# A recommender tower (CIN and three dense layers): group 0 as four batches by 32 columns a tile, its first tile from the first gather alone, w1's quarters sent behind gathers, 17 warm-up products

## The reference

```
e = stack([tbl_0[ids[:, 0]], ..., tbl_31[ids[:, 31]]], axis=1)     # b, field, d
x0 = prev = e
for W in (filter_0, filter_1):                                     # 1024 x 128, 4096 x 128
    z = einsum('bhd,bmd->bhmd', x0, prev).reshape(b, h * m, d)
    prev = relu(einsum('bpd,pn->bnd', z, W[0]))
    outs.append(prev)
z = sum(concatenate(outs, axis=1), axis=-1)                        # b, 256
h = maximum(concatenate([z, dense_ctx], axis=1) @ W_top1 + b_top1, 0)
h = maximum(h @ W_top2 + b_top2, 0)
y = h @ W_top3
```

## Time and profile before

| | |
|---|---|
| median of 3 runs | 834.34 us (833.93 to 834.41) |
| the profiled execution | 833.78 us |
| its span | 832.0 us |
| busy: PE, PE weight load | 825.9 us (99%), 677.7 us (81%) |
| busy: ACT, DVE, POOL | 795.8 us (96%), 789.3 us (95%), 731.0 us (88%) |
| DMA | mean 73 GB/s, 60.91 MB |

### The profile page before, as it was taken

How to read it: one execution, slowest core, us unless ns; L and a number is a source line. 1 busy time by engine, 2 the same in 40 slices (tenths; PEclk the granted TensorE clock), 3 DMA queues, 4 the chain that set the end, 5 groups by cost and what they waited for, 6 DMA issues and landing times.

```text
span 832.0 us, 15690 instructions
## 1 busy us (share of the span) xinstructions
PE 825.9 (99%) x3627; PEld 677.7 (81%) x3627; DVE 789.3 (95%) x2061; ACT 795.8 (96%) x2808; POOL 731.0 (88%) x550
## 2 busy tenths in 40 slices
PE   8999999999999999999999999999999999999999
PEld 6688888888888888888888888888888888888887
DVE  7799999999999999999999999999999999999996
ACT  4799999999999999999999999999999999999995
POOL 5898999989999999999999999999999999999860
PEclk9999999999999999999999999999999999999999
DMA  5541222221233221132331132221122222122000
GB/s 149 180 143 32 66 81 85 86 85 36 63 82 84 84 86 47 51 85 82 84 87 49 48 87 80 84 86 55 43 87 80 86 85 68 33 83 78 1 13 2
DMA packets 62024, 60.91 MB, mean 73 GB/s; under 512 B 26059, under 2 KB 36939, under 8 KB 61934
## 3 DMA queue, kind: packets, MB, share of 16 engines
q1 hardware_dynamic: 57838, 57.80, 23.4%
q0 software_dynamic: 4096, 2.11, 1.6%
HBM read 55.51 MB, written 4.31 MB: 72 GB/s over the span
## 4 chain that ended last, share of the span: by engine, by line
PE 97%; DMA 1%; POOL 1%; issue 0%; SPq 0%; DVE 0%; ACT 0%
PE ps_y L915 28%; PE ps_y L923 28%; PE ps_y L916 28%; PE ps_c L898 3%; PE ps_c L897 3%; PE ps_c L896 3%; POOL gat L452 1%; PE ps_c L894 1%; DMA w_raw<-w 1%; PE ps_c L885 0%; DMA gat<-table,rows 0%; PE ps_y L1019 0%; DMA ids_and_bounds_sb<-ids_and_bounds 0%; POOL w_lo L459 0%; PE ps_y L1021 0%
## 5 line engine op out<-in xcount | busy, mean ns | idle before, releaser
L571 ACT ACTIVATE prod<-ps_y,es 128x128 f32<-128x128 f32 x2560 | 754.1, 647 | 15.8 <-PE ps_y L923 15.6
L740 DVE SCALAR_TENSOR_TENSOR prod<-ps_y,es,prod 128x128 f32<-128x128 f32 x1536 | 422.6, 340 | 28.7 <-PE ps_y L923 26.4
L915 PE MATMUL ps_y<-w_hi,c_both 128*128 128x512 f32 x1024 | 402.8, 393 | 1.0 <-POOL w_lo L459 1.0
L923 PE MATMUL ps_y<-w_hi,c_both 128*128 128x512 f32 x1024 | 398.8, 390 | 0.0
L916 PE MATMUL ps_y<-w_lo,c_both 128*128 128x512 f32 x1024 | 398.6, 389 | 0.0
L441 POOL TENSOR_TENSOR prod<-prod 128x768 f32<-128x768 f32 x128 | 247.1, 1931 | 45.9 <-DVE prod L740 34.2
L752 DVE TENSOR_REDUCE csum<-prod 128x64 f32<-128x896 f32 x256 | 276.5, 1081 | 0.1
L916 PEld LDWEIGHTS ps_y<-w_lo,c_both 128*128 128x128 f32 x1024 | 192.4, 188 | 43.2 <-issue 1.0
L915 PEld LDWEIGHTS ps_y<-w_hi,c_both 128*128 128x128 f32 x1024 | 192.5, 188 | 42.9 <-issue 2.8
L923 PEld LDWEIGHTS ps_y<-w_hi,c_both 128*128 128x128 f32 x1024 | 192.2, 188 | 41.4
L431 POOL TENSOR_TENSOR z<-first,second 128x512 f32<-128x512 f32 x155 | 199.7, 1299 | 0.1
(11 more groups left out here) (122 smaller groups left out, 295.7 us busy)
## 6 DMA issues: line engine op xcount, KB each, us to landing
second<-et_scratch SPq DMA_DIRECT2D x155, 256.0 KB, 4.8
first<-et_scratch SPq DMA_DIRECT2D x31, 256.0 KB, 3.2
et_scratch<-gat SPq DMA_DIRECT2D x62, 64.0 KB
w_raw<-w SPq DMA_DIRECT2D x4, 512.0 KB, 4.7
h_scratch<-h_sums SPq DMA_DIRECT2D x120, 2.0 KB
gat<-table,rows_now POOLq DMA_INDIRECT x116, 2.4
wt_sb<-wt SPq DMA_DIRECT2D x2, 512.0 KB
rows_now<-rows SPq DMA_DIRECT2D x29, 2.0 KB, 1.7
```

The costliest lines, as they stand in the source:

```text
L571: last = nc.scalar.activation(prod[:, buffer_of(g, u), place // 2, :, place % 2], ps_y[:, bank_of(g, u, k), j * N:(j + 1) * N], ACT.Copy, ...
L740: last = nc.vector.scalar_tensor_tensor(out=summed, in0=ps_y[:, bank_of(g, u, k), j * N:(j + 1) * N], scalar=es[:, g.r, u, h:h + 1], in1=s ...
L915: nc.tensor.matmul(out, hi, w_hi, start=True, stop=False)
L923: nc.tensor.matmul(out, lo, w_hi, start=False, stop=True).then_inc(y_ready, 1)
```

## The change

Group 0's columns are ordered in another way: a tile is four batches by all 32 d, so it needs one gather only, and everything of the first tile (spread, picks, multiplies, layer 0) is done on 128 columns from gather 0. The picks of the first tile are fp32 products of unsplit rows; spreading is one multiply of the rows, broadcast, with a 0/1 mask (`own_block`) on DVE. The other three tiles are spread and picked later, on 384 columns, between banks of tile 0. SP asks for w1's first quarter when the first gather has landed, and for the other three together when group 0's other gathers have. POOL takes the remainders of three banks (5, 6, 7) instead of two and issues group 2's gathers behind them. With the new order of columns group 0's sums over d are made in another way (`sum_first`, `sum_h0`). The warm-up has 17 products. Some places in the queues move by one or two banks.

```diff
-WARM_UP = 32
+WARM_UP = 17
...
+LATE_LO = 3
...
+            sp.wait_ge(first_gathered, 16)
             filters(0)
+            sp.wait_ge(gathered[0], rows_gathered(Group(0, 0)))
+            for n in range(1, W1_LOADS):
+                filters(n)
             for s in range(SLOTS):
                 sp.sem_inc(h1_written[s], 16 * BT)
-            sp.wait_ge(gathered[0], 16 * TG)
-            for n in range(1, W1_LOADS - 1):
-                filters(n)
...
             send(Group(0, 1))
-            filters(W1_LOADS - 1)
             fetch(Group(0, 1))
...
-            pool.wait_ge(rows_step, 4)
-            for n in range(FIRST_ROWS):
-                if n == 2 * TG:
-                    pool.wait_ge(first_c_hi, 1)
...
-            for k in (NK - 2, NK - 1):
...
+            pool.wait_ge(rows_step, 4)
+            for n in range(2 * TG):
+                gather_first(n)
+            for k in range(NK - LATE_LO, NK):
...
+            for n in range(2 * TG, FIRST_ROWS):
+                gather_first(n)
...
+            def spread_first():
+
+                dve.wait_ge(first_gathered, 16)
+                shape = [P, BT, D]
+                nc.vector.tensor_tensor(spread[:, FIRST_TILE].rearrange("p (q d) -> p q d", d=D),
+                                        gat[:, 0, 0:D].unsqueeze(1).broadcast_to(shape), own_block.unsqueeze(2).broadcast_to(shape),
+                                        ALU.mult).then_inc(spread_ready, 1)
+                nc.vector.transpose(es[:, 0, 0, :], gat[:, 0, 0:D]).then_inc(first_es, 1)
...
+            def sum_first():
+
+                dve.wait_ge(parts_rectified, 1)
+                dve.wait_ge(h1_written[0], 16 * BT)
+                for u in range(TG):
+                    if u > 0:
+                        dve.wait_ge(first_turned, 2 * u)
+                    nc.vector.transpose(c1_turned[:, :], c1_parts[:, :, u]).then_inc(c1_ready if u == TG - 1 else first_turned, 1)
+                    dve.wait_ge(*((c1_ready, 1) if u == TG - 1 else (first_turned, 2 * u + 1)))
+                    nc.vector.tensor_reduce(h1_sums[:, 0, :].rearrange("p (j b) -> p j b", b=BT)[:, :, u],
+                                            c1_turned[:, :].rearrange("p (j d) -> p j d", d=D), AX.X,
+                                            ALU.add).then_inc(h1_summed if u == TG - 1 else first_turned, 1)
...
-            rest_w1(0)
-            rest_w1(1)
...
+            add_w0()
+            spread_first()
+            split_w0()
             dve.wait_ge(first_copied, 1)
...
-            rest_z(slice(0, 1), first_z_lo, 1)
...
+            rest_z(FIRST_TILE, first_z_lo, 1)
+            rest_w1(0)
+            rest_first(FIRST_TILE, ps_h1, first_c_hi, first_c_lo)
+            rest_w1(1)
+            spread_others()
+            dve.wait_ge(spread_hi_ready, 1)
+            nc.vector.tensor_tensor(spread_lo, spread[:, OTHER_TILES], spread_hi.bitcast(F32), ALU.subtract).then_inc(spread_lo_ready, 1)
+            rest_w0()
+            turn_others()
+            rest_w1(2)
+            dve.wait_ge(first_copied, 2)
+            multiply_others(LASTK)
+            rest_w1(3)
             multiply_others(0)
...
             multiply_others(1)
...
+            rest_w1(4)
```

More of the change, by code:

```diff
@@ L59 @@
 PICK_ORDER = (4, 0, 1, 2, 3)
+PICK_LOADS = ("first",) + PICK_ORDER
+OTHER_PICKS = {"first": 4, 4: 5, 0: None, 1: 4, 2: 5, 3: None}
+LATE_LO = 3
 W1_LOADS = 4
@@ L564, in scale @@
                 if k == ACT_BANKS[u][0]:
-                    if u == 0:
+                    if u == 0 and g.times(1) == 0:
+                        act.wait_ge(first_es, 1)
+                    elif u == (1 if g.times(1) == 0 else 0):
                         act.wait_ge(es_ready, g.times(1, 1))
@@ L584, in _ @@
             nc.scalar.activation(picks_r[:, :, :], picks_sb[:, :, :], ACT.Copy).then_inc(picks_ready, 1)
[L585 to L590, removed]
             act.wait_ge(picked, 1)
-            nc.scalar.activation(first_picked, ps_y[:, PICKS["first"], :], ACT.Copy).then_inc(first_copied, 1)
+            nc.scalar.activation(first_picked[:, FIRST_TILE], ps_y[:, PICKS["first"], FIRST_TILE], ACT.Copy).then_inc(first_copied, 1)
             act.wait_ge(w0_in, 48)
             act.wait_ge(first_z, 1)
-            round_z(slice(0, 1), first_z_hi, 1)
-            round_w1((2, 3))
+            round_z(FIRST_TILE, first_z_hi, 1)
+            round_w1((0,))
             act.wait_ge(l0_first, 1)
             rectify_first(FIRST_TILE, ps_h1, first_c_hi)
-            round_w1((4, 5))
+            round_w1((1,))
+            act.wait_ge(spread_ready, 2)
+            nc.scalar.activation(spread_hi, spread[:, OTHER_TILES], ACT.Copy).then_inc(spread_hi_ready, 1)
+            round_w1((2,))
+            act.wait_ge(picked, len(PICK_LOADS) + 1)
+            nc.scalar.activation(first_picked[:, OTHER_TILES], picks_of_others("first"), ACT.Copy).then_inc(first_copied, 1)
+            round_w1((3, 4, 5))
             def body(g, number):
@@ L622, in body @@
                             rectify_end(u - 2)
-                        if more and (u, k) == (3, 1):
+                        if more and (u, k) == ((3, 3) if number == 0 else (3, 1)):
                             rectify_hi(g.plus(1))
@@ L671, in _ @@
                                         ALU.min).then_inc(rows_step, 1)
[L673 to L679, removed]
@@ L694, in multiply_others @@
             def multiply_others(k):
[L696 to L701, removed]
+                dve.wait_ge(picked, len(PICK_LOADS) + 2 + PICK_ORDER.index(k))
+                multiply_picked(k, OTHER_TILES, picks_of_others(k), z_ready)
@@ L732, in scale @@
                 if k == DVE_BANKS[u][0]:
-                    if u == 0:
+                    if u == 0 and g.times(1) == 0:
+                        dve.wait_ge(first_es, 1)
+                    elif u == (1 if g.times(1) == 0 else 0):
                         dve.wait_ge(es_ready, g.times(1, 1))
@@ L826, in body @@
                             rest_z0(g.plus(1))
-                        if (u, k) == (2, 4) and number != 0:
+                        if (u, k) == (2, 4) and number == 1:
+                            sum_first()
+                        elif (u, k) == (2, 4) and number != 0:
                             add_parts(g.plus(-1))
@@ L841, in body @@
                             turn(g.plus(1))
-                        if more and (u, k) == (3, 3):
+                        if more and (u, k) == ((3, 5) if number == 0 else (3, 3)):
                             rest_c(g.plus(1))
@@ L960, in _ @@
+            pe.wait_ge(w_ready, 1)
             for k in range(LASTK):
```

174 lines of the change are left out of this document (109 added, 65 removed).

## The result

The changed kernel takes 841.86 us (median of 5 runs, 841.74 to 848.8), the kernel before beside it 834.34 (5 runs, 833.68 to 834.94): 1.0109 times as long, interval 1.0092 to 1.0126. It is slower by 7.5 us. Four of the five runs lie between 841.74 and 841.9, one at 848.8. The profiled execution took 841.85, with a span of 840.0 and a mean granted clock of 0.994.

The account below looks back on a forecast made before the run. PE was taken to bound the kernel. The front gives 1.3 us, DVE in group 1 takes 1.0, leaving 0.3: 833.5 us for an execution like the profiled one, 834.0 for the median, range 832.3 to 835.5.

Parts of the forecast that it names:

- Front: Group 0's start: first tile starts 3.6 us sooner; 1.3 us of it left at the end of tile 0.
- quarter two: w1's second quarter, asked for behind the fourth gather near 10.9, lands at 15.1 us; ACT's rounding ends at 15.8.
- G: How much earlier PE starts tile 1's second bank, unless later waits take it back; put at 1.3 us.
- Bank 4's remainder is ready at 19.1: DVE's queue in tile 0: after this moment PE has a closed block of 5.6 us, ending at 24.8.
- POOL late: POOL, with three w1 remainders and gathers behind them, starts its multiplies 2.5 us later; price to PE 0.1 us.
- From there to 62 it can win back its idle time only: DVE, its gain lost by 46.1 us, regains only its idle time up to 62; 0.9 us allowed.
- The four pairs: `sum_first` in group 1: four transposes and four reduces on DVE, net 1.6 us more; PE waits 1.0 us.
- the remainder of z near 76.9: DVE's z remainder for group 3's first product: done at 77.9, wanted at 76.9, so PE waits 1.0 us.
- rival D: Transposes in `sum_first`, with an input stride of four, cost 1.2 us more: 835.2 us; chance 0.10.
- Rival B: `sum_first` doesn't bind, because DVE waits for others in group 1 anyway: 833.1 us; chance 0.25.
- Rival E: TensorE falls to its lower clock in the front's longer sparse stretch: 834.7 to 840 us; chance 0.08.

Follow-up runs that it names:

- experiment 1: Changed kernel, with POOL waiting before the fold of (1,0) until DVE has taken z_lo of group 2's first product; 835.44 us, ratio 1.0014.
- experiment 3: Changed kernel, with DVE's z_lo subtraction for group 2 reading its first input from PSUM instead of SBUF; 834.56 us, ratio 1.0018.
- experiment 5: Kernel before, with only POOL's gathers of group 2 moved behind its w1 remainders (and without its wait for `first_c_hi`); 844.65 us, ratio 1.0149.
- experiment 10: Kernel before, with POOL waiting in groups 1 and 2 for DVE's z remainder for the next group's first product; 834.09 us, ratio 0.9999.
- Experiment 9: On top of experiment 1, w1's third and fourth quarters each asked for only when the one before has landed; 837.95 us, ratio 1.0045.

## Why the prediction was wrong

Forecast 834.0 with a range of 832.3 to 835.5; measured 841.86. Step by step:

- **Front.** First pick 7.4, measured 7.11; first layer-1 product 12.5, measured 12.05; quarter two at ACT about 15.1, measured 15.32. Right.
- **G = 1.3, measured 0.57.** "Bank 4's remainder is ready at 19.1": it began at 18.59 and took 1.22 instead of 0.69, as POOL's first w1 remainder (17.97 to 19.26) ran beside it, and z's took 1.06 instead of 0.55. These two rows are the block in small:

```profile
17.97 1.29 POOL L474 TENSOR_TENSOR w_lo<-w_raw,w_hi 128x512 fp32r<-128x512 f32 x1 [3.95 <-ACT w_hi L599]
20.02 1.29 POOL L474 TENSOR_TENSOR w_lo<-w_raw,w_hi 128x512 fp32r<-128x512 f32 x1 [0.75 <-ACT w_hi L599]
...
18.59 1.22 DVE L845 TENSOR_TENSOR w_lo<-w_raw,w_hi 128x512 fp32r<-128x512 f32 x1
20.66 1.06 DVE L747 TENSOR_TENSOR z_lo<-z,z_hi 128x384 fp32r<-128x384 f32 x1
```

- **POOL late, the step that failed.** POOL's multiplies begin at 27.75 (I said 28.1) against 25.60, DVE waits 1.96 for the first fold, the third fold ends at 45.67 (I said 46.1). All that was right within 0.5, and "From there to 62 it can win back its idle time only" was wrong. I priced POOL's lateness only through what waits for POOL's results, and gave each DVE instruction its duration from the trace of before, whatever POOL did beside it. In its place: 0.24 us of POOL's idle time at 51.4 was what let the subtraction in; without it the subtraction took 7.56 us instead of 0.68, PE lost 5.8, and 2.2 more by the clock. Shown by experiments 1, 3 and 5.
- **The four pairs: 1.0.** The size was right, 1.0 in experiments 1 and 3; the place was not. I let PE wait at the remainder of z near 76.9, and took its margin of 1.0 for the smallest. PE loses half of it 9 us earlier, at a bank of the ring that DVE scales right behind the pairs and its reduce, and most of the rest at later banks. In experiment 1:

```profile
69.46 0.47 PE L992 MATMUL ps_y<-w_hi,c_both 128*128 128x512 f32 x1 [0.22 <-DVE prod L798]
```

  Ahead of it PE is 0.29 early, behind it 0.16 late. With a G of 0.6 in place of 1.3 the forecast's own reckoning would have made this wait 0.3. That it came to 1.0 all the same is luck: those banks bind sooner than the remainder, and the pairs took 2.9 to 3.0 and not 2.6 (a transpose with a stride of four takes 0.41, not 0.30, so rival D had a third of its price). In the changed kernel only 0.54 is seen, as DVE stood ahead of PE again behind the stall. Rival B is out.
- **Rival E.** The clock fell at 12 us, as E had it, and it hardly cost: in the profiled run of experiment 1, whose front has the same instructions and the same 2.31 us of idle time ahead of that product, it stayed at 1.00, and (1,1) starts at 26.33 against 26.48, 0.15 sooner. DVE paces that stretch.

Without the block the changed kernel gives 834.2 to 834.6: the gain of 0.6 in the front, less 1.0 for the pairs. The forecast's sum had 834.0.

## What to carry to other kernels

Before a duration is taken over from an old trace, ask of each DVE instruction with two SBUF inputs what POOL does at that moment, and whether the gap in POOL's row that let it in will still be there: a quarter of a microsecond of idle time was worth seven here. Where PE waits for such an instruction, let POOL wait for it explicitly, in every group and not only where it was seen (this cost nothing measurable in experiment 10; in the changed kernel the subtraction still took 2.1 to 2.2 us), or take one input from PSUM. Only rows of POOL's `TENSOR_TENSOR` were seen to block; other instructions of POOL were not tried. Work that is moved on an engine "off the path" changes its neighbours' durations as well as its own ends.

## What the runs showed that I had not expected

- The block lasts over several POOL instructions: 7.56, 7.57, 7.66, 6.39 and 6.67 us in four kernels, each ending about 0.55 behind the last of an unbroken row on POOL, and 2.1 to 2.2 with a row of two.
- It doesn't touch a subtraction with one input in PSUM (0.68).
- After an idle stretch of PE of 5.65 us the granted clock was 0.50 until 63, for 4.4 us of PE's work, adding 2.2. Behind 2.3 us of idle time it was 0.50 in one profiled run and 1.00 in another.
- In the changed front ACT or DVE can stand 1 to 3 us with all releasers that the profile knows long done, while w1's quarters travel. The times of such kernels lie in heaps. Experiment 9 points to the amount on the way; neither that nor what holds the engine is settled.
